# Sorted tiles for two more expert layers, and results added inside the tile loops, in an eight-block graph and expert network

## The reference, cut to what matters

```python
# level (4 then 8 experts, 1024 hidden); the second level works on the first's output
h = relu(einsum('bsed,edf->bsef', xm, W1) + b1)   # xm: x where chosen, else 0
y = einsum('bsef,efd->bsed', h, W2) + b2
out = sum(y * probs[..., None], axis=2)           # unchosen experts give relu(b1) W2 + b2
# shared and routed (8 experts, 512 hidden)
h_shared = swiglu(flat @ shared_in_w.T)           # times shared_out_w, plus its bias
h_expert = swiglu(flat @ expert_in_w.T)           # one hidden for all experts
# routed: sum over chosen e of (h_expert @ expert_out_weight[e].T * weight + bias[e])
# transformer (8 experts): attention over all tokens with the expert's own weights,
# two norms, 1024 hidden, for the chosen tokens as queries
# normalised (8 experts, 256 hidden)
h = relu(einsum('td,edh->teh', xf, W1) + b1[None])
y = einsum('teh,ehd->ted', h, W2) + b2[None]
y = (y - mu) / sqrt(var + EPS) * gamma[None] + beta[None]
out = sum(gate_w[:, :, None] * y_sel, axis=1)     # gate_w: softmax of the two best logits
```

## Time and profile before

| | us |
|---|---|
| median of 3 runs | 3402.9 (3399.01 to 3406.57) |
| the profiled execution | 3405.7 |
| its span | 3403.9 |
| PE busy in it | 2668.7 (78%) |
| DVE busy | 1654.8 (49%) |
| ACT busy | 1115.8 (33%) |
| POOL busy | 493.6 (14%) |
| DMA, 16 engines | 24% of the span, 72 GB/s |

### The profile page before, as it was taken

The page is one execution under the profiler, slowest core; times in us unless marked ns, Lnnn a source line. Parts: engine busy times, 40 slices in busy tenths (PEclk is TensorE's granted clock), DMA queues, the critical chain, the costliest instruction groups (busy, mean ns, idle before and its releaser), DMA issues. The chain is left out here.

```text
span 3403.9 us, 53143 instructions
## 1 busy us (share of the span) xinstructions
PE 2668.7 (78%) x18883; PEld 2132.7 (63%) x18883; DVE 1654.8 (49%) x3220; ACT 1115.8 (33%) x2110; POOL 493.6 (14%) x758
## 2 busy tenths in 40 slices
PE   6988598599778589965848888888888888734795
PEld 4868598599457344454846677777777777524453
DVE  3636321322247312333427777777777777342353
ACT  2323121122123110001205555555555555223242
POOL 0000122122021000000000111111111111100077
PEclk9989699599689689976979999999999999757797
DMA  4000122244131010021770411442353521120100
GB/s 115 1 7 1 54 87 63 76 126 121 46 91 50 26 56 0 9 41 70 275 256 28 110 59 36 114 115 69 105 134 98 144 75 33 38 50 1 41 25 26
DMA packets 122568, 243.95 MB, mean 72 GB/s; under 512 B 30040, under 2 KB 69682, under 8 KB 118480
## 3 DMA queue, kind: packets, MB, share of 16 engines
q1 hardware_dynamic: 108592, 203.06, 19.2%
q0 software_dynamic: 13728, 37.64, 4.5%
HBM read 451.99 MB, written 53.98 MB: 149 GB/s over the span
## 5 line engine op out<-in xcount | busy, mean ns | idle before, releaser
L2224 PE MATMUL tx_ring<-g_ident,tx_p 128*128 128x128 f32 x2552 | 426.4, 298 | 129.4 <-issue 45.5
L2224 PEld LDWEIGHTS tx_ring<-g_ident,tx_p 128*128 128x128 f32 x2552 | 313.7, 151 | 224.3 <-issue 63.2
L2442 DVE TENSOR_REDUCE tx_neg_max<-tx_scores 128x1 f32<-128x1354 f32 x232 | 362.1, 1561 | 45.4 <-PE tx_scores L2212 45.4
L2449 DVE COPY tx_p_t<-tx_ring 128x512 f32<-128x512 f32 x464 | 306.8, 687 | 134.5 <-PE tx_ring L2224 129.1
L2349 ACT ACTIVATE tx_p<-tx_scores,tx_neg_max 128x1354 f32<-128x1354 f32 x232 | 322.6, 1390 | 96.2 <-DVE tx_neg_max L2442 95.9
L2212 PE MATMUL tx_scores<-tx_keys,tx_queries 96*128 96x512 f32 (+1 forms) x696 | 221.7, 431 | 30.6 <-DMA tx_queries<-tx_q_hi 30.6
L2356 ACT ACTIVATE tx_p_t<-tx_ring 128x384 f32<-128x384 f32 x232 | 113.6, 490 | 356.1 <-PE tx_ring L2224 355.1
L2263 PE MATMUL tx_ring<-tx_p_t,tx_values 128*32 128x128 f32 x5104 | 153.2, 276 | 21.2 <-ACT tx_p_t L2356 20.8
L1297 PE MATMUL sro_ring<-sro_we,sr_h 128*128 128x512 f32 x352 | 155.8, 601 | 6.1 <-DMA sro_we<-_L_ffn_expert_out_weight 6.1
L2263 PEld LDWEIGHTS tx_ring<-tx_p_t,tx_values 128*32 128x32 f32 x5104 | 137.3, 111 | 35.4 <-ACT tx_p_t L2356 34.4
L2212 PEld LDWEIGHTS tx_scores<-tx_keys,tx_queries 96*128 96x128 f32 x696 | 127.7, 212 | 43.2 <-issue 31.0
(11 more groups left out here) (759 smaller groups left out, 5464.9 us busy)
## 6 DMA issues: line engine op xcount, KB each, us to landing
tx_keys<-expert_keys SPq DMA_DIRECT2D x696, 169.5 KB
lv1e_w<-in_L_ffn_W SPq DMA_DIRECT2D x232, 256.0 KB
tx_w<-in_L_ffn_W SPq DMA_DIRECT2D x58, 1024.0 KB
lv0e_w<-in_L_ffn_W SPq DMA_DIRECT2D x200, 256.0 KB
tx_values<-expert_values SPq DMA_DIRECT2D x58, 704.0 KB
tx_rows<-in_L_ffn_rows SPq DMA_DIRECT2D x29, 640.0 KB
g_adj_t<-in_adj_t POOLq DMA_DIRECT2D x4, 3872.0 KB, 22.9
expert_values<-kv_v SPq DMA_DIRECT2D x8, 1408.0 KB, 5.7
```

Source lines behind the costliest of these rows:

```text
L2224: last = nc.tensor.transpose(ring[u % 2][:, (t - t0) * P:(t - t0 + 1) * P], p[n % 2][:, t * P:(t + 1) * P], g.ident[:])
L2442: nc.vector.tensor_reduce(neg_max[:, n % 4:n % 4 + 1], sc[n % 2][:, 0:N], AX_X, ALU.max, negate=True)\
L2449: nc.vector.tensor_copy(p_t[:, n % TURNED, t0:t0 + nt, :], ring[u % 2][:, 0:nt * P].rearrange("p (t q) -> p t q", q=P))\
```

## The change

1. **Combine.** `stage_combine` is gone. A class `Returns` does its work at the end of each tile loop, inside the same block of code: SP loads table and results, TensorE makes the table products in banks of the loop, VectorE adds the weighted results, and POOL, not a product with the identity, adds the sum to g.x. The coefficients are turned in `stage_plan`. The results land in `g.made`, which shares its memory with g.xn and g.xn_t.
2. **Transformer.** SP's first loads have another order.
3. **Routed output.** The dense stage and the bias stage give way to a plan, token-major hidden rows stored to DRAM, and `stage_routed_tiles`: 29 tiles, three weight sets, rows fetched eight tiles ahead.
4. **Normalised experts.** The dense stage and the beta stage give way to a plan and `stage_normed_tiles`, with three weight sets and the same eight tiles.
5. On the host, expert weights are laid out partition by partition; at the start two more blank rows of 1 KB are written.

The core of the diff:

```diff
-def stage_combine(nc, g, tag, plan, acc, table_dram, add):
...
+class Returns:
...
+    def load(self, sync, sent, counts):
+
+        full = N // P
+        for sem, count in zip(sent, counts):
+            sync.wait_ge(sem, count)
+        if self.pads:
+            sync.wait_ge(self.pads_loaded, 16)
...
+    def mix(self, dve, banks):
...
+            dve.wait_ge(self.row_full, b + 1)
+            self.there(dve, b)
+            if self.add and b >= 2:
+                dve.wait_ge(self.summed, b - 1)
+            self.nc.vector.scalar_tensor_tensor(out=self.with_first[0:n, b % 2, :], in0=self.g.made[0:n, b, 0, :],
+                                                scalar=self.plan.share[0:n, b, 0:1], in1=banks[b % len(banks)][0:n, 0:D],
+                                                op0=ALU.mult, op1=ALU.add).then_inc(self.first_done, 1)
...
+    def sum(self, pool):
+        for b in range(NB):
+            n = rows_of(b)
+            pool.wait_ge(self.second_done, b + 1)
+            self.nc.gpsimd.tensor_tensor(self.acc[0:n, b, :], self.acc[0:n, b, :], self.with_second[0:n, b % 2, :],
+                                         ALU.add).then_inc(self.summed, 1)
...
-                pool.wait_ge(sent[k], 16 * ((tiles + 1 - k) // 2))
+                pool.wait_ge(sent[k], all_sent[k])
+            back.load_pads(pool)
+            if add:
+                back.sum(pool)
...
             load_small(0)
             load_weight(0, wq, a["L2_ffn_wq"], wq_loaded)
-            for hd in range(HEADS):
+            load_small(1)
+            for hd in range(2):
                 load_keys(0, hd)
-            for half in range(2):
-                load_values(0, half)
+            stack_queries(0)
+            for hd in range(2, HEADS // 2):
+                load_keys(0, hd)
+            load_values(0, 0)
+            for hd in range(HEADS // 2, HEADS):
+                load_keys(0, hd)
+            load_values(0, 1)
             load_weight(0, wo, a["L2_ffn_Wo"], wo_loaded)
             load_weight(0, w1, a["L2_ffn_W1"], w1_loaded)
             load_weight(0, w2, a["L2_ffn_W2"], w2_loaded)
-            load_small(1)
-            stack_queries(0)
...
+            for b in range(NB):
+                n = rows_of(b)
+                sync.wait_ge(rows_done, b + 1)
+                sync.dma_start(g.hidden_dram[b * P:b * P + n, :], h_rows[0:n, b % 3, :]).then_inc(kept[b % 3], 16)
...
+                for half in range(2):
+                    for k in range(KD):
+                        last = nc.tensor.matmul(wide[b % 2][:, half, :], src_t[:, k, b * P:(b + 1) * P],
+                                                w[1][:, k, half * HID:(half + 1) * HID], start=(k == 0), stop=(k == KD - 1))
...
+def stage_routed_tiles(nc, g, tag, h, shared_dram, expert_dram, plan, bias_dram):
...
+            for i in range(ROUTED_SETS, tiles):
+                sync.wait_ge(done, i - ROUTED_SETS + 1)
+                load(i)
+            back.load(sync, sent, all_sent)
...
+            turn(0)
+            for i in range(tiles):
+                if i + 1 < tiles:
+                    turn(i + 1)
+                project(i)
+            pe.wait_ge(shared_added, NB)
+            back.spread(pe, spare)
...
+            for i in range(tiles):
+                dve.wait_ge(done, i + 1)
+                if i >= 2:
+                    dve.wait_ge(sent[i % 2], 16 * (i // 2))
+                nc.vector.tensor_copy(y[:, i % 2, :], row[i % 2][:, 0:D]).then_inc(y_done, 1)
...
+def stage_normed_tiles(nc, g, tag, w_dram, cols_dram, rows_dram, plan, acc, beta_dram):
...
+            def load(i):
+                k = i % SETS
+                new = dict(cond=expert(i) != expert(i - SETS)) if i >= SETS else {}
...
+            for i in range(SETS, tiles):
+                sync.wait_ge(second_done, i - SETS + 1)
+                sync.wait_ge(out_done, i - SETS + 1)
+                load(i)
+            back.load(sync, sent, all_sent)
...
+            for i in range(tiles):
+                if 0 < i <= tiles - ROWS_AHEAD:
+                    fetch(i + ROWS_AHEAD - 1)
+                pool.wait_ge(out_done, i + 1)
+                send_rows(nc, g, plan, out[:, i % 2, :], i).then_inc(sent[i % 2], 16)
...
+            turn(0)
+            turn(1)
+            first(0)
+            for i in range(tiles):
+                if i + 2 < tiles:
+                    turn(i + 2)
+                if i + 1 < tiles:
+                    first(i + 1)
+                second(i)
+            back.spread(pe, spare + wide)
...
+            result(0)
+            for i in range(tiles):
+                if i + 1 < tiles:
+                    result(i + 1)
+                normalise(i)
+            back.mix(dve, spare + wide)
```

More of the change, by code:

```diff
@@ L113, in _ @@
             sync.dma_start(g.source_dram[N:N + 1, :], g.blank[0:1, :]).then_inc(g.filled, 16)
+            for half in range(HID // D):
+                sync.dma_start(g.hidden_dram[N:N + 1, half * D:(half + 1) * D], g.blank[0:1, :]).then_inc(g.filled, 16)
             sync.dma_start(g.made_dram[0:PADS, :].rearrange("(t p) d -> p t d", p=P),
@@ L1285, in _ @@
             pe.wait_ge(ws_loaded, 16)
[L1286 removed]
             for b in range(NB):
[L1288 to L1299 removed]
+                if b >= 4:
+                    pe.wait_ge(shared_added, b - 3)
@@ new lines, in _ @@
+                for f in range(HT):
+                    last = nc.tensor.matmul(spare[b % 4][:, 0:D], h[:, f, b * P:(b + 1) * P], ws[:, f, :],
+                                            start=(f == 0), stop=(f == HT - 1))
+                last.then_inc(shared_full, 1)
+            turn(0)
[5 more added lines that the diff above has]
+            back.spread(pe, spare)
@@ new lines, in shared_and_routed @@
+            stage_norm(nc, g, "srn", g.xn, g.xn, g.xn_t, affine[:, 0:KD], affine[:, KD:2 * KD])
+            stage_route(nc, g, "srr", g.xn_t, a["L1_ffn_gates"], experts + 2, "grouped", weights, counts,
+                        bias=a["L1_ffn_gate_bias"])
+            stage_plan(nc, g, "srp", weights, counts[:, :, 0:experts], plan, coef=counts)
+        stage_gated_hidden(nc, g, "srh", g.xn_t, a["L1_ffn_shared_in_w"], a["L1_ffn_expert_in_w"], h)
+        stage_routed_tiles(nc, g, "sro", h, a["L1_ffn_shared_out_w"], a["L1_ffn_expert_out_weight"], plan, a["L1_ffn_out_bias"])
@@ L1682, in stage_hidden_tiles @@
         h_act, h_dve, y_done = s.sem("h_act"), s.sem("h_dve"), s.sem("y_done")
+        back = Returns(nc, g, s, plan, acc, b2_dram, add, pads=True)
+        all_sent = [16 * ((tiles + 1 - k) // 2) for k in range(2)]
         block = ctx.enter_context(nc.Block())
@@ L1991, in two_level_experts @@
             with ExitStack() as inner:
-                plan = Plan(Pool(nc, inner, f"lv{level}"), experts, True)
+                plan = Plan(Pool(nc, inner, f"lv{level}"), experts, 2 * experts)
                 with ExitStack() as innermost:
@@ L2200, in _ @@
                     load_weight(i, w2, a["L2_ffn_W2"], w2_loaded)
+            sync.wait_ge(full, at["queries", tiles - 1, 0] + 1)
+            back.load_table(sync)
+            back.load(sync, stored, [16 * ((tiles + 1 - k) // 2) for k in range(2)])
         @block.tensor
@@ L2642, in transformer_experts @@
         experts = a["L2_ffn_wq"].shape[0]
-        plan = Plan(s, experts, False)
+        plan = Plan(s, experts, experts)
         with ExitStack() as inner:
@@ new lines, in normalised_experts @@
+def normalised_experts(nc, g, a):
+    with ExitStack() as ctx:
+        s = Pool(nc, ctx, "ne")
+        experts = a["L3_ffn_Wg"].shape[1]
+        plan = Plan(s, experts, experts)
+        with ExitStack() as inner:
+            t = Pool(nc, inner, "new")
+            weights, mask = t.sb("weights", [P, NB, experts]), t.sb("mask", [P, NB, experts])
+            stage_route(nc, g, "ner", g.xn_t, a["L3_ffn_Wg"], experts, "logits", weights, mask)
+            stage_plan(nc, g, "nep", weights, mask[:], plan, coef=weights, src=g.xn)
+        stage_normed_tiles(nc, g, "nee", a["L3_ffn_w"], a["L3_ffn_cols"], a["L3_ffn_rows"], plan, g.x, a["L3_ffn_beta"])
```

700 lines of the change are left out of this document (380 added, 320 removed).

## The result

The changed kernel takes 3434.1 us in the median of 4 runs (3431.6 to 3439.2), the kernel before 3403.7 beside it: a ratio of 1.0093, interval 1.0075 to 1.0110. That is 30 us more, where the forecast was 19 more. The profiled execution took 3433.9 us (span 3432.2, granted clock 0.852 in the mean, 0.878 before).

A forecast was written before the change was run, and what follows sets the result against it. One core runs stage after stage, so the time is the stages' sum: -25.6-17-42+103.6 = +19, and 3405.7+19-2.8 = 3422 us. Its own range was 3395 to 3450, the whole range 3362 to 3458.

The forecast's parts named there:

- part 4: Normalised experts: plan and sorted blocks take 319.9 us against 216.3 for the bias and expert stages, +103.6 us.
- The ring of part 4: Normalised loop: load, first, second, result, normalise one behind the other, 10.8 us a block with a load, 7.2 without.
- the rule that I had set beside it: Weight loads of the normalised loop: 2.0 us plus bytes over 436 GB/s, 3.2 us for 512 KB; sum 13 us lower.
- My sign of being wrong: Wrong if the last stage's sends come under 9.8 us apart in the mean, or the routed stage takes over 150 us.
- The other signs: Routed sends 2.9 us apart, clock near 0.95; about 24 us from last send to next stage where results are added.
- Part 3: Routed output: sorted stage 131.5 us against 188.0, 2.9 a block; with plan, hidden-stage tail and level 1's seam, -42 us.
- Part 1: Results added inside the loops: level 0 +1.3, level 1 -13.7, transformer -13.2, each with a 4.5 us charge; -25.6 us.
- Part 2: Transformer's first loads reordered: first score some 12 us after the queries are split instead of 29; -17 us.
- The clock stays up: Rival, normalised loop: TensorE needs 2.1 us instead of 3.9 in 25 rings, -45, 3377 us; chance 0.27.
- Returned rows hold the routed loop: Rival, routed loop: copies wait for confirmed sends, 4.05 us a block instead of 2.9, +33, 3455 us; chance 0.18.
- The loads are ahead after all: Rival, normalised loop: POOL's 2.6 us bound a block, 25 rings shrink from 244.8 to 65, 3242 us; chance 0.05.
- POOL's issues are locked out by VectorE's copies: Routed loop: each of POOL's two issues could lose a 0.42 us copy, 3.4 us instead of 2.6; sum 15 us higher.

The follow-up runs named there:

- experiment 7: Changed kernel with six weight sets instead of three and four result buffers instead of two in the routed loop: 3417.4 us, ratio 1.0045.
- experiment 8: Changed kernel with VectorE instead of POOL adding the returned results to g.x: 3426.9 us, ratio 1.0066.
- experiment 9: Changed kernel with SP's first loads in the transformer back in their old order: 3451.7 us, ratio 1.0138.
- experiment 4: Changed kernel with 20 identity turns into a spare bank ahead of each first product in the normalised loop: 3423.9 us, ratio 1.0057.
- experiments 6: Changed kernel with four result buffers instead of two in the routed loop: 3435.0 us, ratio 1.0089.
- experiments 3: Changed kernel, normalised loop: w1 and w2 wait only for the products that last read their buffer, and go ahead of the small loads: 3288.4 us, ratio 0.9654.
- 5: Changed kernel with six weight sets instead of three in the normalised loop: 3268.3 us, ratio 0.9602.
- experiment 12: Changed kernel with six sets in both loops, earlier normalised weight loads, four routed result buffers and adds on VectorE: 3226.4 us, ratio 0.9486.

## Why the prediction was right or wrong, point by point

**The verdict and the size.** Slower was right, and so was the reason: part 4 costs more than the other three bring. 3434 lies 12 us above the 3422 forecast and inside its own range of 3395 to 3450.

**The ring of part 4 was right, in kind and in its steps.** It was read from the waits: no row of before showed such a stage. Forecast 10.8 us with a load; the turn shown took 10.8: VectorE 2.06 (2.2 forecast), SP 0.99 (0.8), load 3.95 (3.9), TensorE 3.79 (3.9, at the low clock). The number of rings was right as well: from block 4 on, 18 with a load and 7 without, and those without took 7.20 (7.2 forecast, though the terms 2.2, 0.8 and 3.9 sum to 6.9; the 0.3 more had no reason stated, and 0.5 us pass between a skipped load and the first product). What was off is one term. Over the 14 rings of which issue and first product are both seen between 3190 and 3350 the load took 4.44 us from the one to the other, not 3.9 (3.69 to 4.93): the row it came from the earlier trace rows had no other transfer beside it, while here a fetch, a send and two small loads go at the same time. That this is the reason was not tested by itself. 18 rings of 11.18 instead of 10.8 make 6.9 of the 7.5 us by which part 4 was too low. By the rule that I had set beside it (the Trainium skill, DMA: Bandwidth & Descriptors, Anatomy of one DMA) the load would take 3.2 us, an estimate. That section is on DMAs issued by GpSimd, and SyncE issues these, so it was not the rule for this load; what the trace shows is 1.2 us more.

One reason for the low clock was misread. I gave level 1's combine as a case of short bursts with gaps, but the earlier trace rows have TensorE busy for 24.55 of its 25 us at a granted 0.50, so that row says nothing of gaps. The level itself came as forecast, 0.60 with both layers mostly at the durations of the low level.

**My sign of being wrong was badly set.** It says that the prediction is wrong if the last stage's sends come less than 9.8 us apart in the mean. Measured are 9.31 over all 28 intervals, so by its words it is met. But the forecast's own 25 rings, 18 of 10.8 and 7 of 7.2, average 9.8 already; 9.8 is where a ring *with* a load would turn the loss into a gain, and in the mean over 25 rings that point lies at 8.8. Measured are 11.18 for rings with a load and 10.06 over the 25; the 9.31 has the short intervals at both ends in it. The mechanism stands, the sign doesn't. The other signs: the routed stage took 137.4 us (under 150), but at a clock of 0.86 over the stage (0.98 in its loop) for the 0.95; from the last send to the next stage 26 to 31 us passed where results are added, not 24.

**Part 3 failed in one place besides small ones.** The pace of the loop was right (2.88 a block, 2.9 forecast) but partly by luck: I put it down to 3.0 us of transfers and 2.6 of POOL, and the mean is 3.03 while rows are fetched and less at the end. In experiment 7 the same work passes at 2.57 a block, so it is POOL's pace when fed, and the rest is the latency of a load behind three sets. That is the same arithmetic as in part 4, which I did not make there. The 8 us missing in part 3 lie outside the loop: 88 shared products 22.2 us instead of 19.4 (+2.8); the end 27.1 instead of 24.2 (+2.9); the hidden stage +7.5 instead of +5 (+2.5). (The outer bound of that loop, 29x(4x0.25+8x0.47), is 138 us and not the 136 written; nothing rests on it.)

**Part 1, right in sum, wrong in cause.** The 5.4 us of the seam before was an open question, and I charged 4.5 us a stage for it, naming a late confirmation or POOL leaving late. Experiment 8 shows the second, and the send is not late (the results' load is issued 2.5 us behind it). It costs 6.2 where POOL adds last, and nothing at level 0, where I charged it too: hence -3.8 there for +1.3, and -10.5 at the transformer for -13.2. The other term that was off is the adding: with POOL adding beside it VectorE's second operation took 0.66 us instead of 0.48, and a block 1.08.

**Part 2, right, with two errors that nearly cancel.** -20.6 at the first score by the trace, -17.6 in the kernel by experiment 9, -17 forecast. The twelve query copies took 7.8 us, not 10 (four in 2.5 to 2.7 instead of 3.35), and the first score started at 1712.1, 9.3 us after the queries were split, where 12 were forecast and 29 were taken before. But 2.6 of the 20.6 us are given back before the first send (156.4 and 138.4 us above), where the forecast gave nothing back.

**The rivals.** *The clock stays up*: no, 0.60 was granted. Forced up by filler (experiment 4) it gave 10 us, not the 45: in the rings with a load the second layer did not follow, and 5 us were lost at the start. The price itself was nearly right, 1.5 us in the rings where both layers ran at the upper level, for the 1.8 forecast. *Returned rows hold the routed loop*: no (experiments 6 and 7), although the list of waits says so. *The loads are ahead after all*: no in the kernel as changed, but it is what experiments 3, 5 and 12 made of it: I had priced it at 3242 from POOL's 2.6 us a block, and six sets came to 3268, all measures together to 3226. *POOL's issues are locked out by VectorE's copies* (the Trainium skill, SBUF — State Buffer, SBUF: two separate sides): POOL's issues took 1.00 and 0.96 us in the loop where VectorE copies each result (0.98 before), and the loop ran at 2.57, their sum with 0.3 of pause each. The 3.4 a block did not come. That doesn't test the rule: that section names copies from SBUF to SBUF, and these read their input from PSUM. In the adding, where both engines compute, one of VectorE's operations did become longer.

## What to carry to other kernels

Count a prefetch ring by its waits, not by its buffers: write down for each load what it waits for, what that waits for, and go round. Three sets of weights are no lead at all when a set is released by a result that itself waits for the next block's products; taking one condition off the weights' wait (with the small loads put behind them) was worth 146 us, a fourth buffer 130. Less work on an engine buys nothing in such a loop. And a profile that blames "issue" or a DMA for a wait gives a suspect: double the buffer it names before believing it.

## What was not expected of the hardware

- After a stage that POOL ended with written-out work some 5 us more pass: 6.2 us to the next stage, against 1.4 where VectorE did the last work (experiment 8), and 0.5 to the store after POOL's hardware loop in the kernel before.
- VectorE's second scalar-tensor-tensor of a block, 128x256 with both large inputs in SBUF, took 0.66 us while POOL added beside it and 0.48 alone. The first, which reads one of them from PSUM, stayed at 0.47 to 0.48. A block took 1.08 us with both engines and 1.37 with VectorE alone, against 0.92 at level 0, where nothing is added.
- One core's transfers reached 333 GB/s over 64 us (experiment 12) and 379 over 45 us (experiment 7). In the ring they moved 92 GB/s at 29% of the engines' time, and each load of 512 KB still took 3.7 to 4.9 us: what that loop lacked was transfers under way, not bandwidth.
- The granted clock followed the feeding: 0.60 in the ring, 0.80 with filler in it, 0.76 with four sets, 0.97 with six, 1.00 with all measures.
